# A two-layer mixer and mixture-of-experts kernel: the front stage written anew, the step size of batch 1 moved between the scans

## The reference

```python
xs = _clamp(_layernorm(xs, norm_w, norm_b))
xz = xs @ in_proj_w.T
xin, z = jnp.split(xz, 2, axis=-1)
xc = causal conv of 4 taps per channel over xin
xc = silu(xc + conv_b)
xdbl = xc @ x_proj_w.T                      # 8 columns for dt, 16 for B, 16 for C
dt = softplus(dt @ dt_proj_w.T + dt_proj_b)
A = -jnp.exp(A_log)
# for each position t:
h = exp(dt_t * A) * h + (dt_t * x_t) * B_t  # 256 channels x 16 states
y = sum over states of h * C_t
y = (y + xc * D) * silu(z)
out = y @ out_proj_w.T
```

## Time and profile before

| | us |
|---|---|
| median of 3 runs | 220.72 (220.1 to 221.04) |
| the profiled execution's own time | 221.12 |
| its span (first to last instruction) | 219.3 |

### The profile page before, as it was taken

One profiled execution on the slowest core, in us unless ns is written; L12 is line 12 of the kernel. 1 busy time (PEld: TensorE's weight loads), 2 busy tenths in 40 slices (PEclk: granted clock), 3 DMA queues, 4 the chain that ended last, 5 costly groups with the idle time before them and its releaser, 6 DMA issues. The chain is left out here.

```text
span 219.3 us, 3893 instructions
## 1 busy us (share of the span) xinstructions
PE 184.9 (84%) x1224; PEld 152.1 (69%) x1224; DVE 144.9 (66%) x339; ACT 122.0 (56%) x279; POOL 109.0 (50%) x140
## 2 busy tenths in 40 slices
...
DMA packets 6148, 9.64 MB, mean 44 GB/s; under 512 B 353, under 2 KB 2930, under 8 KB 6130
## 3 DMA queue, kind: packets, MB, share of 16 engines
...
## 5 line engine op out<-in xcount | busy, mean ns | idle before, releaser
L844 DVE SCALAR_TENSOR_TENSOR acc<-dbx_ps,comb,acc 128x128 f32<-128x128 f32 x96 | 29.4, 345 | 35.9 <-PE dbx_ps L1097 34.6
L325 POOL TENSOR_TENSOR hc<-hs,cb 128x1024 f32<-128x1024 f32 x16 | 37.7, 2357 | 25.3 <-DVE hs L710 25.3
L1073 PE MATMUL bc_ps<-x_hi,w_hi 128*128 128x256 f32 x128 | 41.5, 324 | 0.0
L339 POOL TENSOR_TENSOR w_lo<-w1a,w_hi 128x256 fp32r<-128x256 f32 x32 | 23.8, 749 | 32.5 <-ACT w_hi L524 32.5
L532 ACT ACTIVATE hid<-bc_ps,par 128x256 f32<-128x256 f32 x64 | 26.8, 471 | 21.8 <-PE bc_ps L1075 21.7
L339 POOL TENSOR_TENSOR w_lo<-w1b,w_hi 128x256 fp32r<-128x256 f32 x32 | 23.8, 745 | 27.1 <-ACT w_hi L524 26.9
L710 DVE TENSOR_TENSOR_SCAN hs<-da,dbx_ps 128x1024 f32<-128x1024 f32 x16 | 36.5, 2279 | 0.1
L1075 PE MATMUL bc_ps<-x_hi,w_lo 128*128 128x256 f32 x128 | 36.0, 281 | 0.0
L1074 PE MATMUL bc_ps<-x_lo,w_hi 128*128 128x256 f32 x128 | 36.0, 281 | 0.0
L1097 PE MATMUL dbx_ps<-w2a,hid 128*128 128x128 f32 x256 | 34.1, 276 | 0.5 <-issue 0.3
L1097 PE MATMUL dbx_ps<-w2b,hid 128*128 128x128 f32 (+1 forms) x256 | 33.9, 276 | 0.5 <-DVE acc L844 0.5
...
## 6 DMA issues: line engine op xcount, KB each, us to landing
...
w1b<-w_in SPq DMA_DIRECT2D x2, 1024.0 KB, 12.3
...
w2a<-w_in SPq DMA_DIRECT2D x2, 0.5 KB, 9.2
w2b<-w_in SPq DMA_DIRECT2D x2, 0.5 KB, 10.5
dtw<-dt_rows_in SPq DMA_DIRECT2D x1, 9.0 KB
```

The lines of the kernel that those rows point to most:

```text
L325: nc.gpsimd.tensor_tensor(hc[p][:], hs[p][:], cb[p][:].rearrange("p i (o t) -> p i o t", o=1).to_broadcast([128, PAIR, DC, T]), ALU.mult). ...
L339: nc.gpsimd.tensor_tensor(w1_lo[p][:], w1[layer][:, bass.ds(u * UW, UW)], w1_hi[p][:].bitcast(F32), ALU.subtract).then_inc(s["w1_staged"], 1)
L844: nc.vector.scalar_tensor_tensor(acc[k][:, t, :], o_ps[:, w // span % RING, 128 * t:128 * (t + 1)], comb[layer][b][:, t, bass.ds(u, 1)], a ...
L1073: nc.tensor.matmul(h_ps[:, p, T * c:T * (c + 1)], w1_hi[w][:, at], x_hi[b][:], start=True, stop=False)
```

## The change

- The conv goes to TensorE: the in_proj weights are multiplied by each tap once (`taps`, VectorE, from tap rows that TensorE spreads), and four products over a padded, shifted xs add up (`tapped`).
- dt's two small products become one: w_dt = x_proj(dt columns) times dt_proj, made on TensorE at the start (`rows_out`); the bias is a product with a row of ones.
- Silu is ScalarE's own function. All of conv and z of both batches go through it ahead of the first softplus (`silu1`).
- B and C are computed token by token, copied in fp32 (`bc_copy`), and a row is spread by four transposes of a broadcast column, where there were two bf16 products.
- Batch 1's softplus leaves the front: its B and C columns come after pair 2 (`bc`, `bc_copy` at pair 4), its product v after pair 4, its softplus on ScalarE in pair 5, `rounding` on VectorE and `step_1` on POOL after pair 5, `step_x` on POOL (dtx) after pair 6.
- Decays have four buffers (AHEAD); the loops over pairs are written out.
- The first four weight splits move into batch 1's pairs 0 and 2 (`stage`).
- x is loaded in two halves; two small loads go ahead of the packed parameters.
- Warm-ups stay only before the first scale (three at `rows_out`); those ahead of conv, after B and C, and in softplus go.

The diff, cut to what is spoken of:

```diff
-        plan = [("constants",)]
-        for stage in ("x_stats", "x_norm", "inner_x", "in_proj", "conv", "silu", "x_proj", "softplus", "log"):
-            plan += [(stage, b) for b in range(NB)]
-        plan += [("step_size", 0), ("step_size", 1), ("gate", 0), ("scan", 0, 0, RING), ("scan", 0, RING, NP)]
+        plan = [("constants",), ("x_stats", 0), ("x_stats", 1), ("rows_out",), ("x_norm", 0), ("taps", 0), ("inner_x", 0),
+                ("taps", 1), ("in_proj", 0), ("conv", 0), ("x_norm", 1), ("inner_x", 1), ("conv", 1), ("in_proj", 1),
+                ("z", 0), ("conv1", 0), ("v", 0), ("conv1", 1), ("z_copy",), ("conv1_copy",), ("z", 1), ("bc", 0), ("silu1",),
+                ("softplus", 0), ("bc_copy", 0), ("first_rows",), ("second_b",), ("second_c",)]
+        b1_in = {4: [("bc_copy", 1)]}
+        b1_c = {5: [("softplus", 1)]}
+        b1_out = {2: [("bc", 1)], 4: [("v", 1)], 5: [("rounding",), ("step_1",)], 6: [("step_x",)]}
         for k in range(NP):
-            plan += [("pair_in", k)] + [(name, 0, 0) for name in before_states.get(k, [])] + [("pair_c", k)]
+            plan += [("pair_in", 0, k)] + b1_in.get(k, []) + [("pair_c", 0, k)] + b1_c.get(k, [])
+            plan += [("pair_out", 0, k)] + b1_out.get(k, [])
+        for k in range(NP):
+            plan += [("pair_in", 1, k)] + [(name, 0, 0) for name in before_states.get(k, [])] + [("pair_c", 1, k)]
+            if k in (0, 2):
+                plan += [("stage", k), ("stage", k + 1)]
             if k == NP - 1:
                 plan += [("experts", 0, 0, 0, 1), ("bias2", 0, 0)]
-            plan += [("pair_out", k)] + [(name, 0, 0) for name in after_states.get(k, [])]
-        plan += [("experts", 0, 0, 1, 2), ("last_sum",), ("gate", 1)]
+            plan += [("pair_out", 1, k)] + [(name, 0, 0) for name in after_states.get(k, [])]
+        plan += [("experts", 0, 0, 1, 2), ("last_sum",)]
...
-            sp.dma_start(x_cm[:], x).then_inc(s["x_loaded"], 16)
+            sp.dma_start(x_cm[:, 0, :], x[:, 0, :]).then_inc(s["x0_loaded"], 16)
+            sp.dma_start(x_cm[:, 1, :], x[:, 1, :]).then_inc(s["x1_loaded"], 16)
+            sp.dma_start(row_sb[:], row).then_inc(s["row_loaded"], 16)
+            sp.dma_start(rows_sb[:], rows).then_inc(s["rows_loaded"], 16)
             sp.dma_start(par[:], packed).then_inc(s["params_loaded"], 16)
-            sp.dma_start(dtw[DT0:DT0 + DTR + 1, :], dt_rows).then_inc(s["rows_loaded"], 16)
...
-            def step_size(b):
-                if b == 0:
-                    return
-
-                e, ln = dt_e[:, :, b, :], dt_l[:, :, b, :]
-                pool.wait_ge(s["rounding_dt"], b + 1)
-                pool.wait_ge(s["ln_dt"], b + 1)
-                nc.gpsimd.tensor_tensor(ln, ln, e, ALU.subtract).then_inc(s["log1p_ready"], 1)
-                pool.wait_ge(s["dt_ready"], b + 1)
-                nc.gpsimd.tensor_tensor(dtx[b][:], xc2[:, :, b, :], dt[:, :, b, :], ALU.mult).then_inc(s["dtx_ready"], 1)
...
+            def step_1():
+
+                pool.wait_ge(s["rounded"], 1)
+                pool.wait_ge(s["ln_dt"], 2)
+                link(nc.gpsimd.tensor_tensor(dt_l[1][:], dt_l[1][:], dt_q[1][:], ALU.subtract))
+                nc.gpsimd.tensor_tensor(dt[:, :, 1, :], dt[:, :, 1, :], dt_l[1][:], ALU.add).then_inc(s["dt1_ready"], 1)
+
+            def step_x():
+                pool.wait_ge(s["dt1_ready"], 1)
+                nc.gpsimd.tensor_tensor(dtx[1][:], xc[:, :, 1, :], dt[:, :, 1, :], ALU.mult).then_inc(s["dtx_ready"], 1)
...
+            def rows_out():
+                act.wait_ge(s["wv_ps"], 1)
+                nc.scalar.activation(w_dt[:], halves(wv_ps), ACT.Copy).then_inc(s["wv_ready"], 1)
...
+            def logarithm_table():
+                link(nc.scalar.activation(scrap[:], ones[:, 0:1], ACT.Ln))
...
+                link(nc.scalar.activation(dt_a[b][:], halves(dt_ps[b]), ACT.Abs))
+                if b:
+                    nc.scalar.activation(dt[:, :, b, :], halves(dt_ps[b]), ACT.Relu)
+                nc.scalar.activation(dt_e[b][:], dt_a[b][:], ACT.Exp, scale=-1.0).then_inc(s["exp_dt"], 1)
+                act.wait_ge(s["exp_dt"], b + 1)
+                nc.scalar.activation(dt_l[b][:], dt_e[b][:], ACT.Ln, bias=ones[:, 0:1]).then_inc(s["ln_dt"], 1)
...
+            def silu1():
+
+                act.wait_ge(s["u1_ready"], 1)
+                nc.scalar.activation(xc[:, :, 1, :], u1[:], ACT.Silu).then_inc(s["xc_ready"], 1)
+                act.wait_ge(s["z_copied"], 1)
+                nc.scalar.activation(sz[:, :, 0, :], z0[:], ACT.Silu).then_inc(s["sz_ready"], 1)
+                act.wait_ge(s["z_ps"], 2)
+                nc.scalar.activation(sz[:, :, 1, :], halves(z_ps[1]), ACT.Silu).then_inc(s["sz_ready"], 1)
+                logarithm_table()
...
+            def decays(b, k, q):
+                m = k + NP * b
+                if b == 0 and k == 0:
+                    act.wait_ge(s["a_ready"], 1)
+                if b and k == 0:
+                    act.wait_ge(s["dt1_ready"], 1)
+                if m >= AHEAD:
+                    act.wait_ge(s["h_done"], m + (1 + RING - AHEAD))
+                for c in range(DC):
+                    if b == 0 and k == 0:
+                        act.wait_ge(s["dt0_ready"], c + 1)
+                    for i in range(PAIR):
+                        ins = nc.scalar.activation(da[q][:, i, c, 1:T], dt[:, c, b, 1:T], ACT.Exp,
+                                                   scale=a_neg[:, c * NS + k * PAIR + i:c * NS + k * PAIR + i + 1])
...
+                dve.wait_ge(s["exp_dt"], 1)
+                nc.vector.scalar_tensor_tensor(dt_q[0][:], halves(dt_ps[0]), 0.0, dt_e[0][:], ALU.max, ALU.add)
+                link(nc.vector.tensor_scalar(dt_a[0][:], dt_e[0][:], 1.0, 1.0, ALU.add, ALU.subtract))
+                link(nc.vector.tensor_tensor(dt_q[0][:], dt_q[0][:], dt_a[0][:], ALU.subtract))
+                dve.wait_ge(s["ln_dt"], 1)
+                for c in range(DC):
+                    nc.vector.tensor_tensor(dt[:, c, 0, :], dt_q[0][:, c], dt_l[0][:, c], ALU.add).then_inc(s["dt0_ready"], 1)
+                dve.wait_ge(s["dt0_ready"], DC)
...
+            def rounding():
+
+                dve.wait_ge(s["ln_dt"], 2)
+                link(nc.vector.tensor_scalar(halves(y_ps), dt_e[1][:], 1.0, 1.0, ALU.add, ALU.subtract))
+                nc.vector.tensor_tensor(dt_q[1][:], halves(y_ps), dt_e[1][:], ALU.subtract).then_inc(s["rounded"], 1)
...
+            def tapped(bank, b, c):
+                for k in range(TAPS):
+                    ins = nc.tensor.matmul(bank, w_tap[:, c, k, :], xs[:, b, PAD - TAPS + 1 + k:PAD - TAPS + 1 + k + T],
+                                           start=(k == 0), stop=(k == TAPS - 1))
+                return ins
+
+            def conv(c):
+                pe.wait_ge(s["xs_ready"], 1)
+                pe.wait_ge(s["taps_ready"], c + 1)
+                tapped(conv_ps[c][:, 0:T], 0, c).then_inc(s["conv_ps"], 1)
...
+            def v(b):
+
+                if b:
+                    pe.wait_ge(s["bct_ready"], 2)
+                    bias(b)
+                else:
+                    pe.wait_ge(s["wv_ready"], 1)
+                for c in range(DC):
+                    pe.wait_ge(s["xc_ready"], c + 1 if b == 0 else DC + 1)
+                    for j in range(DC):
+                        ins = nc.tensor.matmul(dt_ps[b][:, T * j:T * (j + 1)], w_dt[:, c, 128 * j:128 * (j + 1)], xc[:, c, b, :],
+                                               start=False, stop=(c == DC - 1 and j == DC - 1))
+                ins.then_inc(s["dt_ps"], 1)
...
 
                 for i in range(PAIR):
-                    row = sel_id[:, bass.ds(k * PAIR + (i + NS * which), 1)]
-                    ins = nc.tensor.matmul(bc_ps[which][:, T * i:T * (i + 1)], row.to_broadcast([SPLIT * BC, 128]),
-                                           parts[:, b, :], start=True, stop=True)
+                    n = k * PAIR + i + NS * which
+                    for t in range(TT):
+                        ins = nc.tensor.transpose(bc_ps[which][:, T * i + 128 * t:T * i + 128 * (t + 1)],
+                                                  bc_tok[:, b, t, n:n + 1].to_broadcast([128, 128]), ident[:])
                 return ins
```

More of the change, by code:

```diff
@@ L49 @@
 BC = 2 * NS
-SPLIT = 3
-XP = SPLIT * BC + DTR
-DT0 = SPLIT * BC
+PAD = 4
+AHEAD = 4
 EXPERTS = (8, 16)
@@ L90, with bass_metaformer @@
 """.split()
-def bass_metaformer(nc, x, packed, dt_rows, w1_0, w2_0, b2, decay, w1_1, w2_1, out):
+def bass_metaformer(nc, x, packed, row, rows, w1_0, w2_0, b2, decay, w1_1, w2_1, out):
     with ExitStack() as ctx:
```

463 lines of the change are left out of this document (194 added, 269 removed).

## The result

| | before | after |
|---|---|---|
| median, us | 220.41 (218.44 to 221.04, 4 runs) | 237.4 (234.69 to 238.67, 4 runs) |
| profiled execution, us (its span) | 221.12 (219.3) | 238.08 (236.2) |

The ratio is 1.0746, with a 95% interval of 1.0617 to 1.0875. Executions of one kernel fall in a faster and a slower state, and every ratio here is of the faster ones alone (three of the four after), which is why it isn't exactly that of the medians. The forecast was 232.5, slower; the sign and the larger cause are right, the size is 4.9 short, and the median lies just above the range's end of 237.

What follows compares the result with a forecast made beforehand. It saw three stages in turn: a front with no engine full, scans bound by VectorE, experts by TensorE. Front 0.0, middle 10.0, smaller terms 0.5, 1.0 and 0.5 made +12.0 us, forecast 232.5, range 226 to 237.

Steps and rivals of the forecast that it cites:

- The step size among the scans: Between scans 4 and 7: batch 1's step size makes VectorE wait for Ln and dtx; loss 10.0 us, bounds 8.5 to 11.5.
- The front: Up to scan 1's end: first scan 2.3 earlier at 35.9, second scan ending as before; gain 0.0, bounds -1.5 and +2.5.
- this ends between 9.9 and 12.3, since the clock rises on the way: TensorE's early queue ahead of batch 0's transposes, from about 4.4: 5.5 us at full clock, twice at half; 10.4 taken.
- The smaller terms: Pair 4's late rows 0.5, half clock after the stall 1.0, moved weight splits 0.5 us.
- Pair 4's rows: TensorE at half clock needs 5.3 per pair over 3.47, so these rows come about 0.5 us late once.
- the long stall: TensorE idles about 3.7, sums of pairs 5 to 7 start at half clock, gate_out waits: +1.0 us (0 to 2).
- the third term: Four weight splits move on POOL from the front to between pairs 8 and 10: about +0.5 us (0 to 1).
- v(1) at half rate: Upper bound of the middle: TensorE does batch 1's step-size product at half clock, 2.7 more; loss stated as 11.5.
- One table set: Rival, 4%: one ScalarE table set holds exp and ln, so loads between them vanish; 227 us, still slower.
- Half rate through the scans: Rival, 6%: B and C row transposes don't hold TensorE's clock up, 1.8 more over some ten pairs; 250 us.
- The cover holds: Rival, 4%: batch 1's step size fits ScalarE's and POOL's idle time, no VectorE idle; 221.7 us (220.2 to 224.2).

Runs made afterwards that it cites:

- e3: The changed kernel with batch 1's step-size products v(1) on TensorE ahead of the sum of pair 3: 234.7 us, ratio 1.065 to the kernel before.
- e4: The changed kernel with POOL's x*dt of batch 1 ahead of the weighting of pair 6 instead of behind it: 234.0 us, ratio 1.067 to the kernel before.
- e5: The changed kernel with the edits of e2, e3 and e4 together: 225.6 us, ratio 1.019 to the kernel before.
- e7: The changed kernel with 128-row products, no table-preload logarithms, and batch 1's step size made in the front: 222.1 us, ratio 1.010 to the kernel before.
- e2: The changed kernel with its products of one and eight rows made as zero-filled products of 128 rows: 232.1 us, ratio 1.057 to the kernel before.
- e9: The kernel before with its 15 front warm-up products made of one row instead of 128: 222.3 us, ratio 1.010 to the kernel before.

## Why the forecast was right in kind and short in size

*The step size among the scans (10.0 forecast, 10.3 measured): right, step by step.* ScalarE idle 4.80 for v(1) (4.4 forecast), VectorE idle 4.83 ahead of the rounding (4.5), decays done 11.26 after scan 4's end (10.95), VectorE idle 3.69 for dtx (3.75), scan 7's end at 20.74 (20.45). e3 and e4 took each wait away alone, e5 both, and e7 the whole.

*The front (gain 0.0 forecast, loss 6.0 measured): the step that failed is "this ends between 9.9 and 12.3, since the clock rises on the way".* It did not rise on the way. The same sentence had the right number beside it, 5.5 at full rate and "twice that at half", which is the 15.7 measured, with its start at 4.17 and 0.6 more. The half rate at the start was taken from the earlier trace rows; there the rise came during 24 full-row warm-ups. The new queue begins with products of one and eight rows, and the forecast has no term for it. e2 and e9 show that it was what decided. Of the 6.0, 5.3 is there when the transposes start, 1.1 comes behind them (e2 takes 0.7 of it away: from the transposes to the first scan 25.88 for 26.56), and 0.4 comes back at scan 1. The forecast's own bound of +2.5 was too near because it gave the half rate only to 12.3. Its mark "wrong, if the first scan starts after 39" was passed.

*The smaller terms (2.0 forecast, 0.6 measured): too high.* Pair 4's rows weren't late (TensorE was back at full rate by about 46: the granted clock is 0.55 from 42 to 46 and 1.00 from 46 to 50). In the long stall TensorE was idle for 5.20 and the next sum took 3.13, at half rate as forecast, but gate_out waited for nothing. Of the third term, the weight splits, 0.6 may be what is left; 1.6 of scatter between executions in that stretch covers it, so it isn't shown.

*Slips in the sums.* 220.7 + 12.0 is 232.7, not 232.5. And v(1) at half rate would by the forecast's own 2.7 make the middle 12.7, not 11.5; with that the range would have ended near 238 and held 237.4, but by luck, since the middle measured 10.3.

*Rivals.* One table set: no, nine loads, also between Exp and Ln in both directions. Half rate through the scans: no. TensorE in the changed kernel, 50 to 66 us (length, busy, granted clock), and from its timeline there a group of transposes and a sum:

```profile
50.00:66.00 16.00, 14.33 (x68) 1.00 0.00 1
```

```profile
57.69 1.11 PE L968 MATMUL bc_ps<-ident,bc_tok 128*128 128x128 f32 x8
59.32 1.98 PE L986 MATMUL m_ps<-hc,ident 128*128 128x512 f32 x4 [0.52 <-POOL hc L326]
```

The granted clock is 1.00, and the pairs follow at 3.45 up to the stall. The 16 us also hold batch 1's B and C products and v(1), but from 56 to 61 TensorE has transposes and sums alone, and they still run at full rate. The Trainium skill, "TensorE: Matmul & The Clock Gate", Part 4, says that transposes don't count as busy for the clock; no run here has transposes without sums between them, so none tests it. The cover holds: no, for the reason given, v(1) came 4.5 after scan 4's end and would have been needed before it.
